# Seven block products in place of eight in a fused attention and feed-forward kernel

## The reference, cut to what matters

```
x = x + layernorm(linear_attention(layernorm(x)))      # causal, chunks of 128 rows
x = x + layernorm(ffn(layernorm(x)))

def ffn(h):                                            # h: [8, 2048, 256]
    q     = h @ W_q.T                                  # 4 heads, two sides of 64
    sim   = q . keys                                   # 64 keys per head and side
    # top 8 of each side, their 64 sums, top 8 of those: indices of experts, scores
    w     = silu((h . down_embed[indices]) * softmax(scores))
    experts = sum of w * up_embed[indices]
    dense = silu(h @ W_up.T) @ W_down.T                # 256 -> 1024 -> 256
    return dense + experts
```

## Time and profile before

| | us |
|---|---|
| median of three runs | 2829.34 |
| span of the profiled execution, first to last instruction | 2828.4 |
| PE busy | 2797.4 |
| ACT busy | 2524.4 |
| DVE busy | 2425.3 |
| POOL busy | 2055.0 |
| mean granted TensorE clock, share of full speed | 0.998 |

### The profile page before, as it was taken

The page is one execution under the profiler, slowest core; times in us unless marked ns, Lnnn a source line. Parts: engine busy times, 40 slices in busy tenths (PEclk is TensorE's granted clock), DMA queues, the critical chain, the costliest instruction groups (busy, mean ns, idle before and its releaser), DMA issues.

```text
span 2828.4 us, 43226 instructions
## 1 busy us (share of the span) xinstructions
PE 2797.4 (99%) x11972; PEld 2179.1 (77%) x11972; DVE 2425.3 (86%) x6125; ACT 2524.4 (89%) x3618; POOL 2055.0 (73%) x2460
## 2 busy tenths in 40 slices
PE   8899999999999999999999999999999999999998
PEld 6678777777777777777777777777777777777777
DVE  5888888888888888888888888888888888888886
ACT  5888999999999989999999999899999999998997
POOL 3777777777777777777777777777777777777675
PEclk9999999999999999999999999999999999999999
DMA  4688878878887888788788878887877888788764
GB/s 116 145 176 173 165 169 176 169 166 175 173 171 162 178 175 166 168 174 174 165 175 174 170 164 177 173 166 171 175 169 165 175 175 170 164 177 170 149 148 121
DMA packets 608757, 471.27 MB, mean 167 GB/s; under 512 B 361859, under 2 KB 543236, under 8 KB 608516
## 3 DMA queue, kind: packets, MB, share of 16 engines
q0 software_dynamic: 52832, 199.77, 39.7%
q1 hardware_dynamic: 555684, 268.74, 38.6%
HBM read 137.37 MB, written 131.20 MB: 95 GB/s over the span
## 4 chain that ended last, share of the span: by engine, by line
PE 89%; POOL 5%; ACT 2%; issue 2%; DVE 2%; DMA 1%; SPq 0%; POOLq 0%; DVEq 0%; ACTq 0%
PE banks L750 83%; PE banks L927 4%; POOL sums L594 3%; PE banks L909 2%; POOL rstd L580 1%; POOL wexp L656 1%; ACT L1113 0%; ACT wexp L1113 0%; POOL cand_best L639 0%; DMA g_parts<-w_way 0%; DVE w_blocks L1275 0%; DVE prob L1260 0%; POOL cdif L659 0%; POOL cprob L608 0%; DVE picked L1202 0%
## 5 line engine op out<-in xcount | busy, mean ns | idle before, releaser
L594 POOL TENSOR_TENSOR sums<-scores 128x1024 f32<-128x1024 f32 x512 | 1008.4, 2060 | 83.2 <-ACT scores L1130 83.2
L580 POOL TENSOR_TENSOR rstd<-var_eps,minus_half 128x1 f32<-128x1 f32 x512 | 512.3, 1001 | 42.7 <-ACT y_sq L1042 15.3
L750 PE MATMUL banks<-deT,xn2T 128*128 128x512 f32 x1024 | 482.7, 594 | 2.6 <-DVE picked L1202 2.2
L750 PE MATMUL banks<-xn2T,wupT 128*128 128x256 f32 (+1 forms) x2272 | 464.8, 359 | 2.5 <-DVE state L1330 2.5
L750 PE MATMUL banks<-wdownT,hT 128*128 128x256 f32 x2048 | 462.9, 379 | 0.8 <-ACT hT L989 0.6
L750 PE MATMUL banks<-ue,gT 128*128 128x256 f32 x2048 | 462.9, 379 | 0.1
L750 PEld LDWEIGHTS banks<-xn2T,wupT 128*128 128x128 f32 x2272 | 398.5, 190 | 51.0 <-DVE state L1330 3.3
L750 PEld LDWEIGHTS banks<-wdownT,hT 128*128 128x128 f32 x2048 | 388.9, 190 | 57.8 <-issue 3.6
L750 PEld LDWEIGHTS banks<-ue,gT 128*128 128x128 f32 x2048 | 388.8, 190 | 53.1 <-ACT gT L1063 0.5
L632 POOL TENSOR_TENSOR wexp<-wexp,w_last 128x1 f32<-128x1 f32 x127 | 126.2, 994 | 347.6 <-ACT z_last L1119 347.6
L750 PEld LDWEIGHTS banks<-deT,xn2T 128*128 128x128 f32 x1024 | 185.2, 191 | 135.2 <-issue 124.2
(11 more groups left out here) (166 smaller groups left out, 6555.0 us busy)
## 6 DMA issues: line engine op xcount, KB each, us to landing
wexp<-wexp POOLq DMA_DIRECT2D x127, 1024.0 KB, 9.4
wexp<-wexp POOLq DMA_DIRECT2D x127, 512.0 KB, 4.5
w_way<-w_blocks SPq DMA_DIRECT2D x127, 512.0 KB, 3.0
g_parts<-w_way SPq DMA_DIRECT2D x508, 128.0 KB, 8.0
xn_way<-xn_blocks SPq DMA_DIRECT2D x992, 32.0 KB, 1.7
x_in<-_attn_hidden_states_dram SPq DMA_DIRECT2D x128, 128.0 KB, 7.0
out_dram<-x_out SPq DMA_DIRECT2D x128, 128.0 KB, 2.8
xn1T<-xn_way SPq DMA_DIRECT2D x125, 128.0 KB, 3.6
```

Source lines behind the costliest of these rows:

```text
L580: return nc.gpsimd.tensor_tensor(rstd[:, n, m:m + 1], var_eps[:, n, m:m + 1], minus_half[:, :], ALU.pow)
L594: return nc.gpsimd.tensor_tensor(sums[:, k, :, :], scores[:, k, 0:XIN].unsqueeze(2).broadcast_to([P, XIN, NKEYS]), scores[:, HEADS + k, :] ...
L750: last = nc.tensor.matmul(out, lhs(c), rhs(c), start=(start and c == 0), stop=(stop and c == chunks - 1))
```

## The change

Three parts, which go together.

1. Tiles 12 to 121 are 55 pairs (a, a+1). The W_down product of a pair is a product of a 2x2 block matrix (two tiles, two halves of the hidden units) with a 2x2 block matrix (two halves of the hidden units, two halves of the 256 columns). Instead of eight products of blocks there are seven, with sums of blocks as operands and sums of products as results. `mix_wdown` makes four sums of W_down blocks once. For each pair POOL makes four 128x512 sums of `hT` blocks (one in the step of t[11] = a, three in the step of t[12] = a), PE seven products of 4 chunks and 128 columns (four in the first step, three in the second; four of the seven go to a separate bank), ACT copies that bank, POOL adds the cross terms (128x128 twice, 128x384 once, at t[13] = a), and DVE adds the bank of y for both tiles in one 128x512 operation at t[14] = a. This replaces the two copies of y on ACT.
2. The mean square, root, output row and store of these tiles come one step later (t[14], t[14], t[15], t[15]); `y_sb` and `x_out` have two buffers.
3. `prob` is no longer a tensor: it is the same memory as `sums`, so the exp overwrites the key sums. Exp h now waits for selection h, and the key sums of a head for the silu of the tile before. To go with that, the mask is made right after weighting head 1, and selection of head 3 moves from the start of the next step to just before weighting head 0; exp 0 comes after the mean square of `mix`. Two staging areas of the setup move to other tensors.

```
+    SEVEN = (PAIRED, LATE - 4)                       # tiles 12 to 121
-        x_out = sb("x_out", [P, D])
+        x_out = sb("x_out", [P, 2, D])
-        prob = sb("prob", [P, HEADS, EXPERTS])
+        prob = sums[:, :, :, :].rearrange("p h x y -> p h (x y)")
+        wdown_mix = sb("wdown_mix", [P, 4, HC, DH])
+        h_mix = sb("h_mix", [P, 2, HC, P])
+        cross = sb("cross", [P, 5, DH])
+        cross_ps = bank[0].rearrange("p (k n) -> p k n", n=DH)

 # POOL
+            def mix_h_upper(a):
+                pool.wait_ge(s_hidden_1_ready, a + 1)
+                pool.wait_ge(s_hidden_0_ready, a + 1)
+                wait(pool, s_y_hidden_in_psum, a)
+                nc.gpsimd.tensor_tensor(h_mix[:, 1, :, :], h_block(a, 0), h_block(a + 1, 0), ALU.subtract).then_inc(s_h_mixed, 1)
+            def mix_h_lower(a):
...
+                nc.gpsimd.tensor_tensor(h_block(a + 1, 0), h_block(a + 1, 0), h_block(a + 1, 1), ALU.add).then_inc(s_h_mixed, 1)
+                pool.wait_ge(s_h_mixed, 4 * nth(a) + 2)
+                nc.gpsimd.tensor_tensor(h_mix[:, 0, :, :], h_block(a + 1, 0), h_block(a, 0), ALU.subtract).then_inc(s_h_mixed, 1)
+                pool.wait_ge(s_h_mixed, 4 * nth(a) + 3)
+                pool.wait_ge(s_y_hidden_in_psum, a + 1)
+                nc.gpsimd.tensor_tensor(h_mix[:, 1, :, :], h_block(a, 1), h_mix[:, 0, :, :], ALU.subtract).then_inc(s_h_mixed, 1)
+            def combine_cross(a):
+                pool.wait_ge(s_cross_copied, nth(a) + 1)
+                nc.gpsimd.tensor_tensor(cross[:, 0, :], cross[:, 0, :], cross[:, 1, :], ALU.add).then_inc(s_cross_steps, 1)
+                nc.gpsimd.tensor_tensor(cross[:, 4, :], cross[:, 2, :], cross[:, 3, :], ALU.add).then_inc(s_cross_steps, 1)
+                pool.wait_ge(s_cross_steps, 3 * nth(a) + 2)
+                nc.gpsimd.tensor_tensor(cross[:, 2:5, :], cross[:, 2:5, :], cross[:, 0, :].unsqueeze(1).broadcast_to([P, 3, DH]),
+                                        ALU.add).then_inc(s_cross_steps, 1)
                 if t[9] is not None:
+                    wait(pool, s_head_3_weights_ready, t[9])
                     key_sums(3).then_inc(s_head_3_sums_ready, 1)
...
+                    if 4 <= t[9] < 8:
+                        mix_wdown(t[9] - 4)
+                if seven(t[13]) and t[13] % 2 == 0:
+                    combine_cross(t[13])
+                if seven(t[11]) and t[11] % 2 == 0:
+                    mix_h_upper(t[11])
+                if seven(t[12]) and t[12] % 2 == 0:
+                    mix_h_lower(t[12])
+                if t[9] is not None:
                     pool.wait_ge(s_head_0_weights_ready, t[9] + 1)
                     pool.wait_ge(s_last_expert_weight, t[9] + 1)

 # PE
+            def seven_products(t):
...
+                if t == a:
...
+                    product(cross_ps[:, 1, :], HC, h_quarter(a, 0), wdown_quarter(0, 0))
+                    y_made(pe, a - 1)
+                    product(y_bank(a)[:, 0:DH], HC, h_quarter(a, 1), wdown_quarter(1, 0), stop=False, shared=True)
+                    product(y_bank(a + 1)[:, 0:DH], HC, h_quarter(a + 1, 1), mixed[3], start=False, stop=False, shared=True)
+                    product(cross_ps[:, 3, :], HC, h_mixed[1], mixed[2]).then_inc(s_y_hidden_in_psum, 1)
+                else:
+                    pe.wait_ge(s_h_mixed, 4 * nth(a) + 4)
+                    product(cross_ps[:, 2, :], HC, h_quarter(a + 1, 0), mixed[0])
+                    product(cross_ps[:, 0, :], HC, h_mixed[0], mixed[1])
+                    product(y_bank(a)[:, DH:], HC, h_mixed[1], wdown_quarter(1, 1), start=False, stop=False, ...)

 # ACT
-                    act.wait_ge(s_head_0_sums_ready, t[9] + 1)
-                    act.wait_ge(s_neg_max_ready, t[9] + 1)
-                    nc.scalar.activation(prob[:, 0, :], head(sums, 0), ACT.Exp, ...)       # now after mix_sq
+                    act.wait_ge(s_head_0_selected, t[9] + 1)
...
-                    act.wait_ge(s_head_1_sums_ready, t[9] + 1)
+                    act.wait_ge(s_head_1_selected, t[9] + 1)
                     nc.scalar.activation(prob[:, 1, :], head(sums, 1), ACT.Exp, ...)
+                if seven(t[13]) and t[13] % 2 == 0:
+                    act.wait_ge(s_y_hidden_in_psum, t[13] + 2)
+                    wait(act, s_pair_y_ready, nth(t[13]))
+                    nc.scalar.copy(cross[:, 0:4, :], cross_ps).then_inc(s_cross_copied, 1)
-                    act.wait_ge(s_head_3_sums_ready, t[9] + 1)
+                    act.wait_ge(s_head_3_selected, t[9] + 1)
-                    act.wait_ge(s_head_2_sums_ready, t[9] + 1)
+                    act.wait_ge(s_head_2_selected, t[9] + 1)
-                if t[12] is not None:
+                if plain(t[12]):
                     act.wait_ge(s_y_in_psum, t[12] + 1)

 # DVE
-                if t[10] is not None:                                  # selection 3, at the start of the next step
-                    dve.wait_ge(s_head_3_sums_ready, t[10] + 1)
-                    nc.vector.scalar_tensor_tensor(picked[:, 1, :], head(sums, 3), ...).then_inc(s_head_3_selected, 1)
+                if seven(t[14]) and t[14] % 2 == 0:                    # before the wait for the numerator
+                    dve.wait_ge(s_y_in_psum, t[14] + 2)
+                    dve.wait_ge(s_x_out_ready, t[14])
+                    dve.wait_ge(s_cross_steps, 3 * nth(t[14]) + 3)
+                    nc.vector.tensor_tensor(y_sb[:, :, 0:D], bank[4]..., cross[:, 1:5, :]..., ALU.add).then_inc(s_pair_y_ready, 1)
                     nc.vector.scalar_tensor_tensor(prob[:, 1, :], picked[:, 1, :], ...).then_inc(s_head_1_weighed, 1)
+                    nc.vector.tensor_tensor(cmask[:, :, :], ...).then_inc(s_cand_mask_ready, 1)
...                                                                    # x_mid
+                    dve.wait_ge(s_head_3_sums_ready, t[9] + 1)
+                    dve.wait_ge(s_head_1_weighed, t[9] + 1)
+                    nc.vector.scalar_tensor_tensor(picked[:, 1, :], head(sums, 3), ...).then_inc(s_head_3_selected, 1)
                     dve.wait_ge(s_head_0_selected, t[9] + 1)
                     dve.wait_ge(s_head_0_prob_ready, t[9] + 1)
                     nc.vector.scalar_tensor_tensor(prob[:, 0, :], picked[:, 0, :], ...).then_inc(s_head_0_weighed, 1)
-                    nc.vector.tensor_tensor(cmask[:, :, :], ...).then_inc(s_cand_mask_ready, 1)
```

More of the change, by code:

```diff
@@ L270, in sandwich_kernel @@
         s_x_out_ready = sem("x_out_ready")
-        s_x_stored = sem("x_stored")
+        s_x_stored = [sem(f"x_stored_{n}") for n in range(2)]
         s_head_0_sums_ready = sem("head_0_sums_ready")
@@ L372, in paired_up, with seven, plain, nth @@
             return PAIRED <= t < LATE
-        def y_bank(t):
-            return bank[{TILES - 3: 5, TILES - 2: 1, TILES - 1: 2}.get(t, 4)][:, 0:D]
+        def seven(t):
+            return t is not None and SEVEN[0] <= t < SEVEN[1]
+        def plain(t):
+            return t is not None and not seven(t)
+        def nth(t):
+            return (t - SEVEN[0]) // 2
+        def y_bank(t):
+            first = D * (t % 2) if seven(t) else 0
+            return bank[{TILES - 3: 5, TILES - 2: 1, TILES - 1: 2}.get(t, 4)][:, first:first + D]
+        def y_made(eng, t):
+            if seven(t):
+                eng.wait_ge(s_pair_y_ready, nth(t) + 1)
+            elif t >= 0:
+                eng.wait_ge(s_y_ready, len([u for u in range(t + 1) if plain(u)]))
+        def wdown_quarter(half, side):
+            return lambda c: wdownT[:, HC * half + c, DH * side:DH * (side + 1)]
+        def h_quarter(t, half):
+            return lambda c: hT[:, t % 4, HC * half + c, :]
         def weights(t):
@@ L540, in _ @@
             pipeline(body)
[L541 removed]
+            for stored in s_x_stored:
+                sp.wait_ge(stored, 16 * (TILES // 2))
         @block.gpsimd
@@ L868, in body @@
                     pe.wait_ge(s_expert_weights_T_ready, t[13] + 1)
-                    product(y_bank(t[13]), EC, lambda c: gT[:, t[13] % 2, c, :], lambda c: ue[:, c, :], start=False).then_inc(s_y_in_psum, 1)
+                    product(y_bank(t[13]), EC, lambda c: gT[:, t[13] % 2, c, :], lambda c: ue[:, c, :], start=False,
+                            shared=seven(t[13])).then_inc(s_y_in_psum, 1)
                 if t[9] is not None:
@@ L1023, in body @@
                     nc.scalar.activation(cdif[:, :, :], cdif[:, :, :], ACT.Exp).then_inc(s_cand_exp_ready, 1)
-                    act.wait_ge(s_head_0_sums_ready, t[9] + 1)
-                    act.wait_ge(s_neg_max_ready, t[9] + 1)
-                    nc.scalar.activation(prob[:, 0, :], head(sums, 0), ACT.Exp, bias=neg_max[:, t[9] % 2, 0:1]).then_inc(s_head_0_prob_ready, 1)
                 if t[7] is not None:
@@ L1183, in xn1_turned, with x_made @@
                 nc.vector.transpose(turned_chunks(xn1_blocks), blocks(xn1[:, :])).then_inc(s_xn1_blocks_turned, 1)
+            def x_made(t):
```

(15 more changed lines are left out.)

109 lines of the change are left out of this document (84 added, 25 removed).

## The result

The changed kernel took 3290.82 us (median of four runs, 3289.24 to 3292.01) against 2829.72 us for the kernel before in the same session: 1.1631 times as long [1.1614, 1.1647]. Slower was right, the size was not: the time lies 141 us above the range.

The account below looks back on a forecast made before the run. The prediction took PE and the DVE and POOL loop as equal bounds, 21.60 us a step. To 2828.4 it added 111 x (23.7 - 21.6) = 233 and 17 x (23.3 - 21.6) = 29: 3090 us, range 2885 to 3150.

Parts of the forecast that it names:

- the loop: Chain from selection 1 through DVE to score masking, then POOL back to selection 1: 21.60 us before, 23.7 forecast in pairs.
- Exps behind selections: Exps 1 and 2 wait for their selections: weighting 1 starts 2.48 us after selection 1, weighting 2 2.50 after selection 2.
- step A: Pair step with POOL's cross sums and one h block: priced at 2.6 us, holding weighting 2 for 0.55.
- selection 1 waits for POOL's sums in nearly every step: Sign expected in the profile after: the selection of head 1 waits for POOL's key sums in nearly every step.
- step B: Pair step with POOL's three lower h blocks: priced at 3.4 us, holding weighting 2 for 0.25, bounds 0 and 1.35.
- What POOL's new place costs: DVE held by POOL: key sums 2 cost weighting 0 1.2 us, blocks cost weighting 2 0.55 or 0.25; loop 23.7.
- DVE operations with two operands in SBUF and POOL's tensor operations exclude each other: Claim that weightings and x_mid are held beside POOL's tensor operations, while selections reading PSUM are not.
- Rows 7: Earlier trace rows: weighting 2 took 3.01 instead of 1.28 us beside POOL's subtractions, weighting 3 1.91 beside key sums.
- I charge nothing for the clock: PE would idle some 2 us per step; its granted clock was expected to stay at 1.00, costing nothing.
- the second: Rival: only the exp order counts, key sums and weighting 0 don't meet; loop 22.1, 64 us more, 2893 us; chance 0.18.
- The third: Rival: weighting 2 waits for POOL's whole block in the 3.4 us step too; loop 24.25, 3152 us; chance 0.15.
- The first: Rival: PE stays the bound, the loop fits into 21.27 us, 37 us saved, 2792 us; chance 0.08.

Follow-up runs that it names:

- e2: The changed kernel without POOL's seven sums per pair (output not the reference's): 3006.12 us, 1.0627 times the kernel before.
- e1: The changed kernel with no pairs, eight products for all tiles, keeping the overwriting exps and new DVE order: 3006.32 us, 1.0628 times the kernel before.
- e7: e1 with weighting 0 moved ahead of the candidate mask, so key sums 2 start behind it: 2994.97 us, 1.0584 times the kernel before.
- e5: The changed kernel with key sums 0 on POOL starting only after weighting 3 of the tile before: 3177.34 us, 1.1227 times the kernel before.
- e6: The changed kernel with 16 extra identity products keeping PE busy in the long wait for masked scores: 3259.13 us, 1.1505 times the kernel before.
- e8: The changed kernel without block sums of h and W_down, with own exp buffers for heads 1 and 2, weighting 0 before the mask: 2818.33 us, ratio 0.9955.
- r1: e1 with DVE reordered: weighting 0 before weighting 1, next row's normalisation before selection 3, two transposes before weighting 2: 2838.24 us, ratio 1.0038.

## Why the prediction was wrong

Right: the loop was the bound and PE's gain was worth nothing (e2 took the time of e1). Exps behind selections: weighting 1 at 2.50 after selection 1 (2.48 worked out), weighting 2 at 2.49 after selection 2 (2.50), the masked scores to selection 1 5.35 in step A (5.37), W_down 3.57 and 2.68 us. Weighting 0 was held by key sums 2, by 0.84 where I took 1.2 of bounds 0 and 1.2, and steps outside the pairs are 22.9 for 23.3. Step A came to 23.85, just what the forecast's terms give for it (23.3 + 0.55), but by luck: the order cost 0.4 less, weighting 2 was not held, and xn2 was, for 0.96. Of the signs, "selection 1 waits for POOL's sums in nearly every step" failed: it waits at the end of step A only (37 of 78 steps between 600 and 2600 us), since step B's loop closes through PE.

The step that failed is "What POOL's new place costs", in its second paragraph: the blocks were charged for weighting 2 alone, 0.4 us a step. What they held was a chain of operations, xn2 in both steps and weighting 2 and weighting 3 in step B, and behind it the clock fell, which the prediction had put at nothing. Per pair the forecast had 47.4 us; 51.2 were measured. The 3.8 us between them, from the rows above:

| term, us per pair | forecast | measured |
|---|---|---|
| weighting 0 held, both steps | 2.40 | 1.68 |
| weighting 2 held, A and B | 0.80 | 0 + 0.62 |
| xn2 held, A and B | 0 | 0.96 + 0.96 |
| weighting 3 held by key sums 0, B | 0 | 1.69 |
| clock after PE's wait, B | 0 | 1.17 |
| loop without these (measured: the rest) | 44.2 | 44.1 |

The rest of 44.1 us fits e1, where a step less its hold is 22.90 - 0.84 = 22.06 us.

- "DVE operations with two operands in SBUF and POOL's tensor operations exclude each other" left out xn2, which has one tensor operand. 1.37 for 0.41 beside a block, and e7's 1.18 for 0.40, show that it is held. The Trainium skill, page "SBUF — State Buffer", section "SBUF: two separate sides", lists VectorE operations "in a 2-port perf mode" beside those with two SBUF inputs; I had used the second half of that sentence. The trace agrees with the first if this operation is in such a mode, which no row shows.
- Rows 7 had shown weighting 3 behind key sums as well; I used them for weighting 0 only. In step A, with xn2 held, weighting 3 still stands 0.56 us ahead of key sums 0 (1419.71 against 1420.27), which come 15.52 us after selection 1 in both steps. The 0.62 us that weighting 2 loses besides in step B use that up: weighting 3 comes 0.05 us behind them and loses 1.69 more. In e5, where key sums 0 wait for it, it is back at 1.24.
- "I charge nothing for the clock" rested on an early stretch with 5.3 us of idle time in 50, a row that does not say how long the pieces are. The wait here is one piece of 4.09 us; e6, which fills it, has the 1.17 us back in step B.
- "POOL itself is not late" holds: in step B it waits 3.55 us for the maxima.

Of the rivals, the second (only the order counts) priced the order at 64 us, without a hold; e1, which has weighting 0's hold in it, puts it at 177. The third foresaw a longer hold in step B, by 0.55 us a step on the mean; it is a chain of holds, of which weighting 3's comes from weighting 2's. The first priced the gain of a free loop at 37 us; e8 had 12, since two unequal steps are not the same as their mean when the next chain lies between them.

## What to carry to other kernels

Before giving work to POOL, list for each of its operations every VectorE operation that may meet it, not only the one due at that time: a hold can delay the next operation into the next POOL operation. In step B here, 0.62 us on weighting 2 grew to 3.27 us of holds, and to 1.17 us of clock. Work that isn't held in these traces (selections that read PSUM, transposes, statistics) is what should stand beside it. A wait that an in-place result brings can be filled by putting other work of the same engine into it, as r1 shows; a saving on an engine that shares the bound is worth only what the next chain leaves.
